# Waits that an engine has already passed are left out, on all five engines of a gated block-sparse LoRA layer

## The reference, cut to what matters

```python
xn = _layernorm(x, axis=-1)                                  # x: (2, 1024, 1024)
bm = mask.reshape(Nb, BH, Kb, BW).sum(axis=(1, 3)) > 0       # 32 x 32 blocks
w = (weight.reshape(Nb, BH, Kb, BW) * bm[:, None, :, None]).reshape(N, K)
s = jnp.einsum('bsk,nk->bsn', xn, w) + bias
base = jnp.einsum('bsi,oi->bso', xn, W_org)
q = jnp.einsum('bi,ki->bk', xn.mean(axis=1), Wq)
coeffs = softmax(jnp.einsum('bk,ek->be', q, lora_keys) / math.sqrt(K))
h = jnp.einsum('bsi,eir->bser', xn, lora_down)
delta = jnp.einsum('be,bser,ero->bso', coeffs, h, lora_up)
x = x + s * _silu(base + delta)
```

## Time and profile before

| what | us |
|---|---|
| median of three runs | 459.79 |
| lowest and highest of them | 459.56, 460.85 |
| the profiled execution, its own time | 461.12 |
| its span, first to last instruction | 459.4 |
| PE busy in the span | 428.3 |
| DVE busy | 350.4 |
| ACT busy | 220.4 |
| POOL busy | 99.1 |

### The profile page before, as it was taken

How to read it: one execution, slowest core, us unless ns; L and a number is a source line. 1 busy time by engine, 2 the same in 40 slices (tenths; PEclk the granted TensorE clock), 3 DMA queues, 4 the chain that set the end, 5 groups by cost and what they waited for, 6 DMA issues and landing times. The chain is left out here.

```text
span 459.4 us, 5836 instructions
## 1 busy us (share of the span) xinstructions
PE 428.3 (93%) x1864; PEld 340.7 (74%) x1864; DVE 350.4 (76%) x487; ACT 220.4 (48%) x390; POOL 99.1 (22%) x90
## 2 busy tenths in 40 slices
PE   1779999999999999988999999998999999999995
PEld 1557676777777787776888788886788887888873
DVE  5797899889879897644568978985856889977624
ACT  3736985186863444222334753434612466544321
POOL 5130356003430200300115023422300110221222
PEclk9999999999999999999999999999999999999999
DMA  8997763277864976979731428669994311546652
GB/s 302 407 345 276 245 209 119 91 247 249 280 224 159 325 223 219 363 250 397 273 93 50 156 93 284 191 211 400 408 385 135 92 51 45 177 151 219 212 201 91
DMA packets 41558, 101.61 MB, mean 221 GB/s; under 512 B 5300, under 2 KB 5300, under 8 KB 40760
## 3 DMA queue, kind: packets, MB, share of 16 engines
q1 hardware_dynamic: 41528, 101.24, 63.6%
HBM read 71.85 MB, written 29.38 MB: 220 GB/s over the span
## 5 line engine op out<-in xcount | busy, mean ns | idle before, releaser
L782 PE MATMUL psA<-b_hi,a_hi 128*128 128x512 f32 x456 | 182.8, 401 | 9.5 <-ACT snaps L996 5.7
L784 PE MATMUL psA<-b_hi,a_lo 128*128 128x512 f32 x456 | 178.6, 392 | 0.0
L783 PE MATMUL psA<-b_lo,a_hi 128*128 128x512 f32 x456 | 178.5, 391 | 0.0
L782 PEld LDWEIGHTS psA<-b_hi,a_hi 128*128 128x128 f32 x456 | 86.0, 189 | 34.9 <-ACT snaps L996 8.3
L784 PEld LDWEIGHTS psA<-b_hi,a_lo 128*128 128x128 f32 x456 | 86.2, 189 | 18.5
L783 PEld LDWEIGHTS psA<-b_lo,a_hi 128*128 128x128 f32 x456 | 86.3, 189 | 16.6
L967 ACT ACTIVATE b_hi<-b_raw 128x512 fp32r<-128x512 f32 (+2 forms) x66 | 45.8, 716 | 53.6 <-DVE b_raw L1113 29.2
L1100 DVE TENSOR_TENSOR b_lo<-b_raw,b_hi 128x512 fp32r<-128x512 f32 (+2 forms) x66 | 52.0, 809 | 10.1 <-ACT b_hi L967 9.5
L1164 DVE TENSOR_TENSOR cst<-psA,snaps 128x512 f32<-128x512 f32 x42 | 28.7, 688 | 29.5 <-ACT snaps L996 17.4
L1100 DVE TENSOR_TENSOR a_lo<-s_raw,a_hi 128x512 fp32r<-128x512 f32 x56 | 43.6, 792 | 6.3 <-ACT a_hi L957 6.2
L996 ACT ACTIVATE snaps<-psA 128x512 f32<-128x512 f32 x42 | 24.9, 594 | 47.6 <-PE psA L784 43.0
(11 more groups left out here) (101 smaller groups left out, 461.2 us busy)
## 6 DMA issues: line engine op xcount, KB each, us to landing
x_nat_sb<-in_x_nat_dram SPq DMA_DIRECT2D x16, 512.0 KB, 5.0
xn_dram<-xq SPq DMA_DIRECT2D x16, 512.0 KB, 5.3
s_dram<-cst SPq DMA_DIRECT2D x32, 256.0 KB, 4.2
worg_sb<-in_w_org_dram SPq DMA_DIRECT2D x32, 256.0 KB, 3.2
xq<-xn_dram SPq DMA_DIRECT2D x16, 512.0 KB, 5.1
s_in<-s_dram SPq DMA_DIRECT2D x32, 256.0 KB, 3.6
xres<-in_x_nat_dram SPq DMA_DIRECT2D x32, 256.0 KB, 4.1
out_dram<-cst SPq DMA_DIRECT2D x32, 256.0 KB, 4.0
```

The source lines that it names most:

```text
L782: nc.tensor.matmul(ps, l_hi, r_hi, start=first, stop=False, skip_group_check=True)
L783: nc.tensor.matmul(ps, l_hi, r_lo, start=False, stop=False, skip_group_check=True)
L784: return nc.tensor.matmul(ps, l_lo, r_hi, start=False, stop=over, skip_group_check=True)
```

## The change

Each engine's handle is wrapped in an object that remembers, for each semaphore, the highest value that this engine has waited for. A wait for a value that is not higher emits nothing. Semaphores of this kernel only count up, so such a wait was always met when it was reached. Nothing else differs: the steps, their order, their operands and what each adds to a semaphore are the same.

```diff
+class Waits:
+
+    def __init__(self, eng):
+        self.eng, self.reached = eng, {}
+        self.dma_start = eng.dma_start
+
+    def wait_ge(self, sem, value):
+        if self.reached.get(sem.name, 0) < value:
+            self.reached[sem.name] = value
+            self.eng.wait_ge(sem, value)
+
...
         @block.sync
         def _(sp):
+            sp = Waits(sp)
...
         @block.tensor
         def _(pe):
+            pe = Waits(pe)
...
         @block.scalar
         def _(act):
+            act = Waits(act)
...
         @block.vector
         def _(dve):
+            dve = Waits(dve)
...
         @block.gpsimd
         def _(pool):
+            pool = Waits(pool)
```

## The result

The changed kernel took 463.44 us in the median of 22 runs (460.59 to 466.89), the kernel before 461.0 us in 22 runs beside them (459.3 to 464.38). The ratio is 1.0053, with a 95% interval of 1.0036 to 1.0071: slower by 0.5%, some 2.4 us. The prediction was no change, 459.6 us, and slower by over 0.3% had a chance of 0.04. It was wrong.

The account below looks back on a forecast made before the run. The prediction took PE's matmul count and spacing to bound the kernel. Savings of 0.05 (PE), 0.1 (SP) and 0.05 (an unnamed hand-over) made 0.2 us, so 459.79 - 0.2 = 459.6 us, range 458.6 to 460.4 us.

Parts of the forecast that it names:

- What bounds the kernel: Whole kernel: outside the start and a few short stops, PE's matmul count and spacing set the end; PE busy 93%.
- PE, 0.05 us: PE's list: 101 wait instructions hidden by its queue, one bare place assumed; 0.05 us saved, bounds 0 and 0.2.
- the rival of waits on the path: PE's stream: each wait instruction delays it, so 101 x 0.051 = 5.2 us would go, giving 454.6 us; chance 0.03.
- Bias matmuls, 0: PE's bias matmuls: 0.40 us lost at each blamed on shape, so 0 gained; 7.6 us kept as rival, chance 0.03.
- DVE 0: DVE's list: its wait instructions run under other work, so removing them gains 0.
- SP 0.1: SP's load burst from 201.49 us: five wait instructions fewer, earlier issue saves 0.1 us, bounds 0 and 0.28.
- SP's gaps in the burst: Sign to look for ahead of line 721's loads on SP: gaps of 0.05 instead of 0.11 us.
- The wait for `d_snaps`, 1.2 to 1.5 us: PE's stop until 215.64 us, 1.47 us long: expected at 1.2 to 1.5 us; above 1.8 would mean loads bunched up.
- The slower rival: SP's loads behind the second `d_snaps` load bunch up on full DMA engines; PE's stop grows 2.7 us, 462.5 us; chance 0.04.
- PE's other waits within 0.1 us: Sign in the changed profile: PE's listed waits stay at the same places, each within 0.1 us.
- The clock: PE's clock over the whole span: read as granted in full in all 40 slices.
- The range: Total time: 459.0 to 459.8 us widened for the median's error and run spread to 458.6 to 460.4 us.

Follow-up runs that it names:

- e17: The changed kernel with one met wait instruction added ahead of each of PE's 65 steps between 52 and 206 us; 461.23 us, ratio 1.0006.
- e16: The kernel before with 101 met wait instructions added in one lump ahead of PE's first step; 463.64 us, ratio 1.0053.
- e18: The kernel before with 184 met wait instructions added, up to three ahead of each PE step between 52 and 206 us; 463.33 us, ratio 1.0073.
- e7: The kernel before with repeated waits removed from PE's list alone, and only the two of nineteen bias matmuls; 460.55 us, ratio 0.9995.
- e3: The kernel before with repeated waits removed from DVE's list alone, 65 wait instructions fewer; 461.16 us, ratio 1.0001.
- e1: The kernel before with repeated waits removed from SP's list alone, 81 wait instructions fewer; 460.21 us, ratio 1.0000.
- e14: The same kernel as e2, run again in a later job against the kernel before; 463.6 us, ratio 1.0062.
- e2: The kernel before with repeated waits removed from PE's list alone, 101 wait instructions fewer; 463.14 us, ratio 1.0061.

## Why the prediction was wrong

- **What bounds the kernel:** right. PE is busy 93% of the span after as before.
- **PE, 0.05 us:** the handling was right. The matmuls are 0.23 us apart with and without wait instructions among them, and e17 puts 65 back for +0.06% (-0.21 to +0.34). The size of one was misread: a bar of 51 ns isn't its cost, since 101 in a row start 0.106 us apart (e16), so that the rival of waits on the path was worth 101 x 0.106 = 10.7 us and not 5.2; even 0.106 fits under 0.23. But this is the step that failed: I costed the wait instructions as work of the sequencer and not as room in PE's code. With 55 to 101 gone, a code fetch falls into the flight of one store, which lands after 3.4 to 4.5 us instead of 2.1 to 2.6, and PE's stop at 317 us is 2.8 us instead of 1.4. The sentence "whatever goes was already met, so nothing that blocks today is unblocked by it" is true of the semaphores only. Missing was a term of about 2.4 us that comes or goes with the place of the code: 65 instructions more take it away (e17), 184 more bring it (e18). The page showed its cause (q8, 15 packets), and the trace of before showed how near it was: 6.6 us.
- **Bias matmuls, 0:** right (e7, and 0.31, 0.43 and 0.34 us in the trace after). That the two rows of weights are the reason for the 0.40 us wasn't tested; only the waits are ruled out.
- **DVE 0, SP 0.1:** right within what can be measured (e3, e1). SP's gaps in the burst of the earlier trace rows fell to 0.04 us, as foreseen:

```profile
200.94 0.80 SPq L734 DMA_DIRECT2D b_hi<-d_dram  x2
201.78 0.62 SPq L734 DMA_DIRECT2D d_snaps<-d_dram  x1
202.44 1.07 SPq L754 DMA_DIRECT2D temp<-in_up_dram  x2
```

- **The wait for `d_snaps`, 1.2 to 1.5 us:** wrong, it was 0.35 us after, but it swings anyway: 1.45 us in e14, where SP's list is that of before. A gain there is given back at 317 us, since that stop ends by a load and not by PE.
- **The slower rival** was the right kind, a transfer in another's way that ends in a stop of PE, and the wrong pair: loads of SP against each other. e1 gives 1.0000 for it.
- **PE's other waits within 0.1 us:** wrong, and the long stop at 317 us should have been asked about. I read that the six waits for ACT were 5.7 us together, and not what the longest hung on: a load, behind a store, behind a transfer for which DVE waits 0.45 us, with little slack: when the store lands 2.1 to 2.6 us after its issue, the load of `xq` follows 10.5 to 10.7 us behind PE's 1181st matmul, and when it takes 3.4 us or more, 11.8 to 12.6 us.
- **The clock:** I took it as full, since all 40 slices of one execution were. The 17 to 35 runs beside the experiments have it at 0.9932 to 0.9937 in the mean, and a longer stop of PE can cost a drop on top of itself.
- **The range:** 458.6 to 460.4 us came from three runs; the spread of 22 runs of the same kernel is 459.3 to 464.4.

ACT's and POOL's lists weren't tried alone; e2 and e14 leave nothing for them to explain that these intervals could show.

## What to carry to other kernels

Removing instructions that cost nothing moves the fetches of an engine's code against the data transfers, and a stage in which a wait for a store or load has little slack can turn that into some tenths of a per cent, in either direction. When an edit has a loss that no half of it has, look for something that hangs on how much was changed and not on what, and test the place of the code by hidden padding that is spread under full queues; padding in one lump lies bare, and costs more than its bars. Ahead of a "no change", look for the waits for transfers that are short but end a chain into the bounding engine, and give them a price for being late.

## What was new about the hardware

- PE's code comes in 15 packets of 16 KB on q8 in this kernel (16 with 184 instructions more), each 0.9 to 2.8 us long. With one in the flight of a 256 KB store the store lands after 3.4 to 4.5 us instead of 2.1 to 2.6: fifteen of its sixteen counts come as ever and the last one 1.5 us behind the end of the packet.
- 65 wait instructions spread one for a step cost nothing that can be measured; 101 in one place have bars of 51 ns but start 0.106 us apart, and delayed PE's first matmul by 5.6 us.
- The granted clock falls to the lower level for 3.4 us (twice that in a row in some traces) in or just behind stops of PE of 1.85 to 3.3 us. Not each such stop has a drop (2.60 us at 317 us in the changed kernel has none), and the same kernel has it in one execution and not in the next: the kernel before shows no drop in one trace and two in the other (28.6 and 199.3 us).
- Around a matmul with two rows of weights among such with 128 PE loses 0.40 us, with or without waits (0.32, 0.43 and 0.34 us instead of 3 x 0.23 in e7 as in the kernel before).
